# Softmax attention's front: Pool's two norm products wait for the split, and the dummy products are issued in two parts

## The reference

```python
def block5(x):                      # x: (2, 1024, 128), already layer-normed once by the caller
    x_norm = layer_norm(x, g1, beta1)
    q, k, v = heads(x_norm @ Wq + bq), heads(x_norm @ Wk + bk), heads(x_norm @ Wv + bv)
    q, k = rope(q) / sqrt(8), rope(k)
    attn = softmax(q @ k.T)
    x = x + (attn @ v) @ Wo + bo
    return x + relu(layer_norm(x, g2, beta2) @ W1 + b1) @ W2 + b2
x = x + block5(layernorm(x))
```

## Time and profile before

| | |
|---|---|
| runs without a profile | 1016.04, 1023.14 and 1021.83 us, median 1021.83 |
| the profiled execution | 1019.93 us |
| its span | 1018.1 us |
| mean granted clock of PE | 0.928 |
| busy: PE, DVE, ACT, POOL | 816.8, 694.2, 530.6 and 185.3 us |

### The profile page before, as it was taken

How to read it: one execution, slowest core, us unless ns; L and a number is a source line. 1 busy time by engine, 2 the same in 40 slices (tenths; PEclk the granted TensorE clock), 3 DMA queues, 4 the chain that set the end, 5 groups by cost and what they waited for, 6 DMA issues and landing times.

```text
span 1018.1 us, 15314 instructions
## 1 busy us (share of the span) xinstructions
PE 816.8 (80%) x5607; PEld 493.5 (48%) x5607; DVE 694.2 (68%) x1324; ACT 530.6 (52%) x1139; POOL 185.3 (18%) x177
## 2 busy tenths in 40 slices
PE   4889734999988678888888788887798689895893
PEld 2578533699855342111111121211266489585693
DVE  6844882366488989999999988896143455557363
ACT  1530442165434466788888877787655145124252
POOL 2000037355402300000000000000030635103452
PEclk9999956999999789999999999998899699996897
DMA  4730001411210000000000000000050121100213
GB/s 114 214 105 1 1 13 52 123 37 35 78 34 1 1 1 1 1 1 1 1 1 2 1 1 1 2 1 1 1 166 1 42 81 35 47 1 19 88 35 103
DMA packets 54139, 36.73 MB, mean 36 GB/s; under 512 B 9186, under 2 KB 49314, under 8 KB 54066
## 3 DMA queue, kind: packets, MB, share of 16 engines
q1 hardware_dynamic: 49298, 25.98, 9.2%
q0 software_dynamic: 4768, 9.77, 2.9%
HBM read 22.31 MB, written 13.43 MB: 35 GB/s over the span
## 4 chain that ended last, share of the span: by engine, by line
PE 43%; issue 24%; DVE 12%; ACT 10%; POOL 6%; DMA 3%; SPq 2%; DVEq 0%; POOLq 0%; ACTq 0%
PE psum L1523 13%; PE psum L1511 9%; ACT arena L1672 7%; POOL results L1004 6%; PE psum L248 3%; PE psum L1085 3%; DVE arena L1463 2%; PE psum L1440 2%; PE psum L1095 2%; PE psum L359 2%; PE psum L337 2%; PE psum L394 1%; PE psum L241 1%; DVE stats L164 1%; SPq L860 1%
## 5 line engine op out<-in xcount | busy, mean ns | idle before, releaser
L1463 DVE TENSOR_REDUCE arena<-psum 128x2 f32<-128x1024 f32 x256 | 298.3, 1217 | 25.7 <-PE psum L1440 24.8
L1672 ACT ACTIVATE arena<-psum 128x512 f32<-128x512 f32 x512 | 264.6, 603 | 77.2 <-PE psum L1511 77.2
L1511 PE MATMUL psum<-arena 32*128 32x512 f16 x512 | 117.6, 387 | 64.9 <-ACT arena L1672 63.6
L1128 ACT ACTIVATE arena<-psum,arena 128x128 f32<-128x128 f32 x340 | 97.2, 369 | 114.6 <-PE psum L1095 63.1
L1523 PE MATMUL psum<-arena 128*32 128x512 f32 x1024 | 139.0, 615 | 0.1
L1511 PEld LDWEIGHTS psum<-arena 32*128 32x128 f16 x512 | 29.5, 91 | 224.4 <-ACT arena L1672 201.2
L248 PE MATMUL psum<-la_wqkv,ident 128*128 128x384 f32 x320 | 117.3, 517 | 11.4 <-DVE arena L1902 8.5
L1440 PE MATMUL psum<-arena 32*128 32x512 f16 x512 | 109.1, 384 | 7.2 <-ACT arena L1782 4.5
L1004 POOL DMA_INDIRECT results<-arena x85 | 84.4, 993 | 108.5 <-DVE arena L1287 103.9
L996 POOL DMA_INDIRECT slots<-xn,arena x64 | 66.4, 1037 | 203.3 <-DVE arena L1205 184.7
L1085 PE MATMUL psum<-arena 128*128 128x128 f32 x680 | 95.1, 284 | 0.7 <-DVE arena L1282 0.6
(11 more groups left out here) (272 smaller groups left out, 1025.6 us busy)
## 6 DMA issues: line engine op xcount, KB each, us to landing
arena<-slots SPq DMA_DIRECT2D x19, 256.0 KB, 3.0
arena<-results SPq DMA_DIRECT2D x16, 256.0 KB, 3.9
slots<-blank SPq DMA_DIRECT2D x1, 2560.0 KB, 12.3
expert_w<-in_L_attn_b_w_dram SPq DMA_DIRECT2D x1, 2048.0 KB, 8.5
expert_w<-in_L_attn_b_w_dram SPq DMA_DIRECT2D x8, 256.0 KB, 5.1
expert_w<-in_L_ffn_W_dram SPq DMA_DIRECT2D x1, 2048.0 KB, 8.4
expert_w<-in_L_ffn_W_dram SPq DMA_DIRECT2D x8, 256.0 KB, 5.2
results<-arena POOLq DMA_INDIRECT x85
```

The costliest lines, as they stand in the source:

```text
L1128: last = nc.scalar.activation(self.hT[:, p, c, :], ps[:, 2 + p, c * P:(c + 1) * P], self.func, bias=own[:, FF + c:FF + c + 1])
L1463: v.tensor_reduce(self.mx[:, h % 2, keys, qt, 2 * pair:2 * pair + 2], core.psum[:, 2 * slot:2 * slot + 2, :], AX.X, ALU.max).then_inc(self ...
L1511: nc.tensor.matmul(core.psum[:, 4 + tile % self.SCORE_BANKS, :], self.kT[rows, g, at:at + P], self.qT2[rows, h % 2, :], start=True, stop=T ...
L1672: nc.scalar.activation(self.prob[:, k % self.PROBS, j, :], core.psum[:, 4 + tile % self.SCORE_BANKS, :], ACT.Exp).then_inc(self.prob_in, 1)
```

## The change

It makes two edits. On PE, the nine dummy products behind the wait for `high_in` become four ahead of it and three behind it. On POOL, the work on `xn` starts only when `split_in` has reached 2 (`B` is 2), that is when DVE has finished the split of both halves, the last thing that it does ahead of the loop.

```diff
--- before.py
+++ after.py
@@ -1702,8 +1702,9 @@
         pe.wait_ge(self.pads, 3)
         pe.wait_ge(w.ident16_in, 1)
         core.claim(pe, self.t[0]["qkT"][0])
+        keep_busy(core, w, pe, self.t[0]["qkT"][0].bank, 4)
         pe.wait_ge(self.high_in, 1)
-        keep_busy(core, w, pe, self.t[0]["qkT"][0].bank, 9)
+        keep_busy(core, w, pe, self.t[0]["qkT"][0].bank, 3)
         pe.wait_ge(self.again_in, 1)
         pe.wait_ge(self.split_in, 1)
         for i in range(8):
@@ -1938,6 +1939,8 @@
         for b in range(B):
             ts = slice(b * TB, (b + 1) * TB)
             pool.wait_ge(self.normed, b + 1)
+            if b == 0:
+                pool.wait_ge(self.split_in, B)
             mean, r = (core.ln[:, i, ts].unsqueeze(2).to_broadcast([P, TB, D]) for i in (0, 4))
             core.pstep(g_.tensor_tensor(core.xn[:, ts, :], core.x[:, ts, :], mean, ALU.subtract))
             core.pstep(g_.tensor_tensor(core.xn[:, ts, :], core.xn[:, ts, :], r, ALU.mult))
```

## The result

| | before | changed |
|---|---|---|
| median of the runs | 1018.93 us (1014.64 to 1023.14, 4 runs) | 1009.10 us (1005.27 to 1014.22, 4 runs) |
| ratio, 95% interval | | 0.9893 (0.9855 to 0.9930) |
| span of the profiled execution | 1018.1 us | 1012.4 us |
| mean granted clock of PE | 0.928 | 0.932 |

The account below looks back on a forecast made before the run. The front was taken as a serial prefix, mostly DVE, then PE's dummies and ACT's copies: 7.25 (POOL's holds) - 0.3 (L1874) + 3.8 (bound passing to DVE) = 10.7 us off 1020.9 us, giving 1010.2 us, range 1004.5 to 1016.

Parts of the forecast that it names:

- the start of the maxima: Start of DVE's unbroken run of row maxima at the ring, 369.07 us before: to come 10.7 us earlier.
- POOL's holds: DVE's L171, L174 and L1885 to L1887 ahead of high_in wait for POOL operations; moving POOL's work saves 7.25 us.
- 0.3 us at L1874: DVE's earlier L1874 of half 0 meets PE's last projection at its eighth operation, giving back 0.3 us.
- rival (c): In half 0's rotation, something else, such as ACT's pad fills, lengthens L1885 to L1887; only 3 us won, 1017.9 us; chance 0.06.
- The maxima beside POOL: Some eight row maxima run beside POOL's moved work; delay bounded by nothing and 12.3 us, taken as nothing.
- The rule of the Trainium skill: POOL contends with DVE instructions in 2-port perf mode or with two SBUF inputs; by it the maxima run free.
- Rival (a): At 355 to 368 us POOL holds the maxima up, costing 12.3 us against 10.7 won: 1022.5 us; chance 0.07.
- Dummies and copies: PE's seven dummies let transposes start at 344.1 us instead of 356.15; ACT's copies end at 354.1 us.
- The step from a bound by ACT to one by DVE: At the ring's start, DVE's second split at 355.2 us becomes the bound instead of dummies and ACT's copies: 3.8 us.
- The ring's first turn at the low clock: PE's first turn takes 3.1 us from 355.2 us, so the maxima run from 358.3 us.
- Rival (b): PE's clock stays low: 14 dummy instructions at 1.2 GHz, ring 1.8 us late, gain 7.9 us, 1013.0 us; chance 0.07.
- A second slow turn: Two ring turns at the low clock instead of one would cost some 1 us.

Follow-up runs that it names:

- e3: Changed kernel, but POOL starts behind the first split instead of the second; ratio to the kernel before 0.9999 (0.9973 to 1.0025).
- e4: Changed kernel without the seven dummies in front of the transposes; ratio to the kernel before 0.9893 (0.9860 to 0.9925).
- e5: Changed kernel plus four dummies on PE between the first half's transposes and the ring's first fills; ratio to the kernel before 0.9925 (0.9895 to 0.9955).
- e7: Changed kernel plus two dummies on PE behind the ring's first two fills; one execution, no ratio, stretch from L164 to L1468 62.11 us.
- e8: Changed kernel plus six dummies between the first half's transposes and the ring's first fills and four behind those; ratio to the kernel before 0.9879 (0.9842 to 0.9915).
- e9: The changed kernel's code run once more, nothing altered; ratio to the kernel before 0.9880 (0.9839 to 0.9921).
- e1: Changed kernel with POOL's edit only, all nine dummies again behind the wait for high_in; ratio to the kernel before 0.9897 (0.9865 to 0.9929).
- e2: Changed kernel with the split dummies only, POOL working where it did before; ratio to the kernel before 0.9980 (0.9952 to 1.0008).

## Why the prediction was right

Forecast 1010.2 us (1004.5 to 1016.0), measured 1009.10 us; forecast 10.7 us off the start of the maxima, measured 10.68 us (369.07 - 312.18 = 56.89 us before, 362.77 - 316.56 = 46.21 us after). The mechanism is borne out term by term. That the sum agrees to 0.02 us, and the time to 1.1 us, is partly luck: at L1468 the same code gained 10.66 us in one profile and 9.92 in the other, and the changed kernel's four runs lie from 1005.27 to 1014.22 us.

- **POOL's holds, 7.25 us, less 0.3 us at L1874.** Measured 6.96 us at the high parts, with 0.26 us lost at L1875: its eighth operation waited for the first projection, which took 7.09 us on PE. In e3, e4, e5, e7, e8 and e9 that projection took 5.40 us, L1875 ran without a pause, and the high parts came at 28.12 to 28.15 us. So the 0.3 us hangs on PE's clock, and without it the holds are 35.36 - 28.13 = 7.23 us. e1 shows the term alone (28.39 us), e2 the opposite (35.36 us), and e3 that the hold goes with POOL's place and not with half 0, which settles rival (c). One reading under this term was wrong: L174 is counted among the operations with two SBUF sources, but it is a TENSOR_SCALAR of one source. Its 1.61 us were right; the kind of operation that POOL holds was drawn too narrowly, as L1902 and L210 show. e2 is also what rival (c) describes, high parts late and dummies divided: it won 3.70 us at the ring where (c) has 3, since (c) kept ACT as the bound.
- **The maxima beside POOL, bounded by 0 and 12.3 us, taken at nothing.** Their range of durations is unchanged at 1210 to 1226 ns, with POOL running from 359.76 to 372.30 us. Rival (a) is out. The reading from L1874 carried over: neither it nor the maxima were held, and both read PSUM. The reason that the prediction adds, one source fewer, carries nothing, since L174 with a single source was held. A source in PSUM isn't the only way to be free either: the statistics (L164) read SBUF and weren't held.
- **The rule of the Trainium skill** ("GPSIMD Engine Reference", "Key points"). The runs agree for its second class, two SBUF inputs (L1887 in e3, 2.92 us for 1.22), and for the maxima, which are in neither. For its first class, the 2-port perf mode, they fit but don't show it: L1902 was held in e3 (2.71 us for 0.69) and does its 1024 columns in 0.69 us, against 1.22 for the products, but no row names the mode that it runs in.
- **Dummies and copies.** Transposes at 344.1 us expected, 312.18 + 31.57 = 343.75 us measured on the same scale: the lower bound. I had allowed a few instructions at the low clock; none was (2.82 us for eight and 2.20 us for six). It cost nothing either way: ACT's slack was expected at 1.1 us (354.1 against 355.2 us) and measured at 1.0 us.
- **The step from a bound by ACT to one by DVE, 3.8 us.** Measured alone in e2: 3.70 us.
- **The ring's first turn at the low clock, 3.1 us.** Measured 3.06 us. Rival (b) has two parts. All 14 dummy instructions at the low clock, and a ring that waits for ACT because of it, came up in no profile. A second slow turn did: its dummy took 1.55 to 1.65 us in e2, e3, e4, e5 and e9, and DVE paused 0.3 to 0.9 us more, where I had said some 1 us. Its 0.92 us in e9, less the 0.26 us at L1875, are most of the difference between the 62.19 and 62.93 us of one code.
- **Why the time was 1.1 us off.** The runs of the kernel before differ more than that among themselves: their median is 1018.93, 1020.21, 1016.15 and 1022.49 us in four sets. From the first of these, the forecast's 10.7 us would have given 1008.2 us. What makes the untouched blocks differ (627.8 to 640.0 us behind L1468 in eleven profiles) was not studied and stays open.

## What to carry to other kernels

When a vector operation on SBUF is two or three times as long as its twin, look at what POOL does beside it: if its end follows POOL's end by about its own normal duration (here 1.08 us, with 1.22 us alone), it was held. Then move POOL's work beside operations that read PSUM, rather than cutting it into pieces. Dummy products must not stand behind the wait that sets the path (3.7 us here), and whether they are needed at all is decided by the next engine: here ACT's copies took 7.43 us whether the transposes ran at the high or the low clock.

## What the hardware showed that I had not expected

- POOL also holds DVE operations with one SBUF source that write to SBUF (L1902: 2.71 us for 0.69; L210: 3.42 us for 2.14, eight of them), while the statistics (L164) take 1.64 us beside POOL and alone. The kernel before had shown it already: L174, 1.78 us for 0.17, is such an operation.
- The hold is mutual: a POOL operation of 1.89 us takes 2.74 us beside DVE's products, and a piece of 0.40 us takes 1.26 us.
- An eighth of a POOL operation of 1.90 us costs 0.40 us, not 0.24 us.
